# A mixture-of-experts router on four column tiles, and one transpose for a supertile's weights

## What is computed

```python
x = x + attn(layernorm(x))                 # latent attention, 64 sequences of 64 tokens, 8 heads
x = x + moe1(layernorm(x), ctx)            # 8 experts of width 512, top 2, routed by ctx
x = x + moe2(layernorm(x))                 # the part that the change touches

def moe2(h):                               # h: (4096, 128)
    scores = sigmoid(h @ gate_w.T)         # 32 experts
    sc = scores + gate_bias
    grp = sc.reshape(-1, 8, 4)             # 8 groups of 4; keep the 4 groups with the best top-2 sum
    gmask = one_hot(top_k(top_k(grp, 2).sum(-1), 4)).sum(1)
    tki = top_k(where(repeat(gmask, 4) > 0, sc, 0), 8)
    w = scores[tki]; w = w / (w.sum(-1) + 1e-20) * 2.5
    combine = (one_hot(tki, 32) * w).sum(1)          # (4096, 32)
    g, u = silu(h @ w_gate), h @ w_up                # every token through every expert, width 64
    routed = (g * u * combine) @ w_down
    return routed + silu(h @ sh_gate) * (h @ sh_up) @ sh_down   # a shared expert of width 128
```

## Time and profile before

| | |
|---|---|
| time, median of 3 runs | 756.46 us (754.01 to 759.85) |
| profiled execution | 756.52 us, of which 754.8 us from its first to its last instruction |
| TensorE busy | 669.3 us, 89% of the span |
| VectorE busy | 552.5 us, 73% |
| ScalarE, GpSimd busy | 353.1 us, 47%; 345.7 us, 46% |
| mean granted TensorE clock | 0.95 |
| second expert layer | from about 400 us to the end |

### The profile page before, as it was taken

One profiled execution on the slowest core, in us unless ns is written; L12 is line 12 of the kernel. 1 busy time (PEld: TensorE's weight loads), 2 busy tenths in 40 slices (PEclk: granted clock), 3 DMA queues, 4 the chain that ended last, 5 costly groups with the idle time before them and its releaser, 6 DMA issues.

```text
span 754.8 us, 11001 instructions
## 1 busy us (share of the span) xinstructions
PE 669.3 (89%) x3456; PEld 475.5 (63%) x3456; DVE 552.5 (73%) x1318; ACT 353.1 (47%) x628; POOL 345.7 (46%) x386
## 2 busy tenths in 40 slices
PE   6868999999708999999992988999999999999997
PEld 5535666666506777777771755666666666666664
DVE  4367877779517999999964786777868695958564
ACT  3844666655204666666663533444343424353221
POOL 5111377778867999999957324040312213000000
PEclk9967999999958999999997898999999999999999
DMA  9900300000023466666311293354555545444442
GB/s 227 366 11 0 92 30 29 29 29 34 38 77 88 127 206 193 179 188 193 113 56 45 59 207 87 90 154 109 132 112 138 129 112 132 111 130 112 124 116 58
DMA packets 73816, 84.14 MB, mean 111 GB/s; under 512 B 15057, under 2 KB 42683, under 8 KB 73758
## 3 DMA queue, kind: packets, MB, share of 16 engines
q1 hardware_dynamic: 68536, 74.93, 36.4%
q0 software_dynamic: 4096, 8.40, 3.8%
q10 hardware_dynamic: 1126, 0.11, 0.1%
HBM read 64.48 MB, written 18.87 MB: 110 GB/s over the span
## 4 chain that ended last, share of the span: by engine, by line
PE 57%; POOL 18%; DVE 11%; issue 7%; ACT 4%; DMA 2%; another core or an unknown queue 0%; SPq 0%; POOLq 0%; ACTq 0%; DVEq 0%
PE pair_banks L1625 15%; POOL h1h L586 7%; PE bank L1408 7%; PE bank L1410 6%; PE bank L1409 6%; POOL W2l L571 4%; PE pair_banks L1315 4%; PE score_banks L1410 3%; PE score_banks L1408 3%; PE score_banks L1409 3%; POOL W2h L566 3%; PE bank L1447 2%; PE pair_banks L1493 2%; POOL x_sorted L544 2%; PE bank L1467 2%
## 5 line engine op out<-in xcount | busy, mean ns | idle before, releaser
L865 ACT ACTIVATE r_s<-bank 128x512 f32<-128x512 f32 x136 | 81.1, 598 | 160.7 <-PE bank L1410 150.8
L1625 PE MATMUL pair_banks<-t_s,Dn 128*128 128x512 f32 x272 | 138.6, 595 | 0.0
L1150 DVE TENSOR_TENSOR h1l<-r,h1h 128x512 fp32r<-128x512 f32 x92 | 113.4, 1251 | 16.2 <-POOL h1h L586 16.2
L1408 PE MATMUL bank<-fxh,Gh 128*128 128x512 f32 x136 | 97.6, 718 | 0.0
L1265 DVE TENSOR_TENSOR rc_s<-r_s,score_banks 128x512 f32<-128x512 f32 x90 | 61.5, 684 | 49.0 <-ACT r_s L865 39.5
L1278 DVE TENSOR_TENSOR t_s<-rc_s,bcb 128x512 f32<-128x512 f32 x128 | 87.4, 685 | 4.1 <-DMA bcb<-c_rows 2.6
L586 POOL TENSOR_SCALAR h1h<-r 128x512 fp32r<-128x512 f32 x92 | 73.8, 806 | 19.6 <-ACT r L816 17.3
L605 POOL TENSOR_TENSOR mvp<-mvp,meps 128x4 f32<-128x4 f32 x8 | 1.6, 197 | 172.4 <-DVE mvp L1188 172.4
L544 POOL DMA_INDIRECT x_sorted<-xsb,posi x64 | 64.2, 1003 | 31.9 <-DVE xsb L1077 19.8
L597 POOL DMA_INDIRECT yg<-y_sorted,posi x64 | 64.3, 1005 | 25.3 <-issue 18.4
L1625 PEld LDWEIGHTS pair_banks<-t_s,Dn 128*128 128x128 f32 x272 | 51.4, 190 | 14.7 <-issue 3.8
(11 more groups left out here) (286 smaller groups left out, 1611.4 us busy)
## 6 DMA issues: line engine op xcount, KB each, us to landing
bcb<-c_rows SPq DMA_DIRECT2D x128, 256.0 KB
wraw<-in_L_xattn_W SPq DMA_DIRECT2D x46, 256.0 KB, 2.9
x_sorted<-wraw SPq DMA_DIRECT2D x1, 5888.0 KB, 17.4
xg<-x_sorted SPq DMA_DIRECT2D x23, 256.0 KB, 3.4
y_sorted<-ysb SPq DMA_DIRECT2D x23, 256.0 KB, 3.0
ctxb<-in_ctx SPq DMA_DIRECT2D x8, 256.0 KB, 6.0
out<-x_all SPq DMA_DIRECT2D x8, 256.0 KB
x_all<-in_x SPq DMA_DIRECT2D x2, 512.0 KB, 5.2
```

The costliest lines, as they stand in the source:

```text
L865: act.activation(r_s[:, n % RB2, :], bank[n % 3][:, :], ACT.Silu).then_inc(F["act"], 1)
L1150: tt(h1l[:, n % NB1, :], r1[:, n % RB1, :], h1h[:, n % NB1, :].bitcast(F32), ALU.subtract)\
L1408: mm(dst, wh, xh, start=start, stop=False)
L1625: mm(bank[6][:, :], Dn[:, weights_of(p), :], t_s[:, n % TB2, :], start=(p == 0), stop=(p == NC2 - 1))\
```

## The change

The router logits of the second layer take the form of the first router: `gwT` is stationary, tokens stream, the four tiles of a supertile go to four column tiles. The result, experts of four tiles on 128 rows by 128 tokens, is copied to SBUF (`lgS`, a new step of ScalarE), and turned by one transpose (`back`, a new step of TensorE) before the sigmoid. The routing weights `cw` (128 x 4 tiles x 32) are turned by one 128x128 transpose in place of four; `cT` is 128x128, and SP writes it to `c_rows` in four DMAs. In the tables, `sc` and the routing of supertiles 2 to 7 come one chunk later; supertile 1's `lg` comes one chunk later, `sc`, `rt_a` to `rt_d`, `c_ps` and `cT` two chunks later (`rt_a` from chunk 11 to 13, `c_ps` from 16 to 18, which is chunk 1 of supertile 1). In the first expert layer the bias load counts on the weights' semaphore.

```diff
-SLOTS = dict(cmbA=-5, cmbB=-4, paggr=-3, prstd=-2, pnb=-1, pxn=0, pxT_ps=2, pxT=2, fxl=3, lg=4, sc=5, rt_a=6, rt_b=7,
-             rt_c=8, rt_d=9, c_ps=14, cT=14, accS=8, tp=10, x2=12)
-
-
-FIRST = dict(cmbB=4, paggr=4, pnb=5, pxn=7, pxT_ps=9, pxT=9, fxl=10, lg=11, sc=11, rt_a=11, rt_b=12, rt_c=13, rt_d=14,
-             c_ps=16, cT=16)
+SLOTS = dict(cmbA=-5, cmbB=-4, paggr=-3, prstd=-2, pnb=-1, pxn=0, pxT_ps=2, pxT=2, fxl=3, lg=4, lgS=4, back=5, sc=6, rt_a=7,
+             rt_b=8, rt_c=9, rt_d=10, c_ps=14, cT=14, accS=8, tp=10, x2=12)
+
+
+FIRST = dict(cmbB=4, paggr=4, pnb=5, pxn=7, pxT_ps=9, pxT=9, fxl=10, lg=12, lgS=12, back=13, sc=13, rt_a=13, rt_b=14, rt_c=15,
+             rt_d=16, c_ps=18, cT=18)
...
-    steps = [(name, 1) for name, s in FIRST.items() if i == 0 and s == p]
+    steps = [(name, 1) for name, s in FIRST.items() if divmod(s, NC2) == (i, p)]
...
-            cT = a("cT", [E2, ST])
+            cT = a("cT", [P, P])
+            lgS = a("lgS", [P, P])
...
-                sp.dma_start(bcur[:, b % BB, :].unsqueeze(1), bT[:, ds(e, 1), :]).then_inc(s_b[b % BB], 16)
+                sp.dma_start(bcur[:, b % BB, :].unsqueeze(1), bT[:, ds(e, 1), :]).then_inc(s_w[b % WB], 16)
...
-                sp.dma_start(cs[j], cT[:, :]).then_inc(s_cs, 16)
-                sp.wait_ge(s_cs, 16 * (j + 1))
+                for t in range(TPS):
+                    sp.dma_start(cs[j][:, t * P:(t + 1) * P], cT[t * E2:(t + 1) * E2, :]).then_inc(s_cs, 16)
+                sp.wait_ge(s_cs, 16 * TPS * (j + 1))
...
-                    pool.wait_ge(s_w[b % WB], 32 * (b // WB + 1))
+                    pool.wait_ge(s_w[b % WB], 48 * (b // WB + 1))
...
+            def prep_lg(j):
+                act.wait_ge(F["lg"], j + 1)
+                copy(lgS[:, :], bank[7][:, 0:P]).then_inc(F["lgS"], 1)
+
             def prep_sc(j):
-                act.wait_ge(F["lg"], j + 1)
-                act.activation(scores[:, :, :], bank[7][:, 0:TPS * E2].rearrange("p (t e) -> p t e", t=TPS),
+                act.wait_ge(F["back"], j + 1)
+                act.activation(scores[:, :, :], bank[7][:, P:P + TPS * E2].rearrange("p (t e) -> p t e", t=TPS),
                                ACT.Sigmoid).then_inc(F["sc"], 1)
 
             def prep_c(j):
                 act.wait_ge(F["c_ps"], j + 1)
                 if j >= 1:
-                    act.wait_ge(s_cs, 16 * j)
-                copy(cT[:, :], bank[7][0:E2, :]).then_inc(F["cT"], 1)
+                    act.wait_ge(s_cs, 16 * TPS * j)
+                copy(cT[:, :], bank[7][:, 0:P]).then_inc(F["cT"], 1)
...
                 for t in range(TPS):
-                    ins = mm(bank[7][:, t * E2:(t + 1) * E2], xTt[:, t * P:(t + 1) * P], gwT[:, :],
+                    ins = mm(bank[7][t * E2:(t + 1) * E2, 0:P], gwT[:, :], xTt[:, t * P:(t + 1) * P],
                              start=True, stop=True)
                 ins.then_inc(F["lg"], 1)
+
+            def prep_back(j):
+                pe.wait_ge(F["lgS"], j + 1)
+                transpose(bank[7][:, P:2 * P], lgS[:, :]).then_inc(F["back"], 1)
 
             def prep_c(j):
...
-                for t in range(TPS):
-                    ins = transpose(bank[7][0:E2, t * P:(t + 1) * P], cw[:, t, :])
-                ins.then_inc(F["c_ps"], 1)
+                transpose(bank[7][:, 0:P], cw[:, :, :].rearrange("p t e -> p (t e)")).then_inc(F["c_ps"], 1)
 
             prep_x(0)
             prep_logits(0)
             pe.wait_ge(s_f2l, NG)
+            prep_back(0)
```

More of the change, by code:

```diff
@@ L299, in decoder_kernel @@
         s_w = [sem(f"expert_in{i}") for i in range(WB)]
-        s_b = [sem(f"expert_bias_in{i}") for i in range(BB)]
         s_xg = [sem(f"sorted_in{i}") for i in range(XB)]
@@ L323, in decoder_kernel @@
         F = {n: sem("f2_" + n) for n in (
-            "up gate act rc t dn accS tp x2 cmb1 cmb bst pstat prstd pnb pxn pxT_ps fxh xT fxl lg sc cw c_ps cT "
+            "up gate act rc t dn accS tp x2 cmb1 cmb bst pstat prstd pnb pxn pxT_ps fxh xT fxl lg lgS back sc cw c_ps cT "
             "chain").split()}
@@ L811, in _ @@
                 if c == 0:
-                    act.wait_ge(s_b[b % BB], 16 * (b // BB + 1))
+                    act.wait_ge(s_w[b % WB], 48 * (b // WB + 1))
                 act.wait_ge(B["up"], n + 1)
@@ L858, in _ @@
             prep_x(0)
+            prep_lg(0)
             prep_sc(0)
@@ L879, in _ @@
                             prep_x(j)
+                        if name == "lgS":
+                            prep_lg(j)
                         if name == "sc":
@@ L1676, in _ @@
                             prep_logits(j)
+                        if name == "back":
+                            prep_back(j)
                         if name == "c_ps":
```

## The result

| | before | after |
|---|---|---|
| median | 756.68 us (753.54 to 759.85, 15 runs) | 749.34 us (747.27 to 751.2, 15 runs) |
| profiled execution | 756.52 us, span 754.8 | 747.27 us, span 745.5 |
| TensorE busy, VectorE busy | 669.3, 552.5 us | 660.7, 552.1 us |
| first transpose of the second layer to the end | 342.40 us | 335.47 us |

The ratio is 0.9907 with an interval of 0.9889 to 0.9925: 7.0 us less, against 8.0 forecast. It is 0.93%, so by the bound of 1% named in the prediction "the same".

What follows compares the result with a forecast made beforehand. TensorE was taken to bound the second expert layer's steady part. From the profiled 756.5 us, -6.0 (chunk 18), +2.1 (clock) and -4.1 (steady supertiles) sum to -8.0: 748.5 us forecast, range 743.5 to 753.5.

Steps and rivals of the forecast that it cites:

- the hole before supertile 1's weights: TensorE's wait for VectorE's `cw` before transposing supertile 1's weights: 3.2 us in place of 5.1.
- the hole at 438: TensorE's idle time from 437.58 to 439.24, supertile 1's logits waiting for `fxl`: claimed to close.
- Chunk 18 earlier, -6.0: Second chunk of supertile 1: first product at 457.5 in place of 463.53, 6.0 us earlier.
- The clock, +2.1: TensorE's clock falls to half after the 3.2 us wait before supertile 1's weights, losing 1.7 to 2.9 us, taken as 2.1.
- Rival A: Clock holds through the shorter wait before supertile 1's weights, so no 2.1 us loss: 746.4 us, chance 0.17.
- Steady, -4.1: Supertiles 2 to 7: cheaper logits and transposes on TensorE save 0.68 us each, 4.1 us in all (3.2 to 4.9).
- Rival D: Column tiles and transposes save little, as switching from full width costs more: 750.9 us, or 752.6 with nothing saved; chance 0.08.
- First spread, d = +0.5: Supertile 0's routing weights, written and broadcast: net 0 to 1.0 us later, taken as 0.5, from three more write issues.
- Rival C: The four DMA writes run one after another, delaying the first spread by 4.0 us: 752.0 us, chance 0.07.
- Rival B: Wait before supertile 1's weights does not shrink, VectorE 2 us later through late gathers or broadcasts: 750.5 us, chance 0.14.
- Rival E: TensorE idles at each supertile's transpose back, waiting for ScalarE's late copy: slower, 759.7 us at 3.5 us lateness, chance 0.05.
- The bias semaphore: First expert layer: GpSimd's `w_high` waits for a third small load, three blocks ahead: costs nothing.

Runs made afterwards that it cites:

- before's second trace: The kernel before, unchanged, profiled once more: 751.07 us, 338.78 us from the second layer's first transpose to the end.
- the shift alone: Kernel before with only supertile 1's step table moved later (logits before chunk 12, transposes before 18), old logits and transposes kept: 750.59 us, ratio 0.998.
- the filler: Changed kernel with 23 unused 256-column products on TensorE before it waits for supertile 1's weights: 745.27 us, ratio 0.9912 to the kernel before.
- The run with doubled products: Changed kernel with the four column-tile logits products issued twice: steady supertile period 40.12 us in place of 39.90.
- the change again: The changed kernel, unaltered, run again on the second chip: 746.63 us, ratio 0.9932 to the kernel before.
- the two tables alone: Kernel before with supertile 1's steps shifted and later supertiles' combines behind the routing, old logits, transposes and single write kept: 745.38 us, ratio 0.9907.
- the later combine: Changed kernel with the combine of the next supertile but one, and preparation steps after it, moved behind the routing: 742.64 us, ratio 0.9883 to the kernel before.

## Why the prediction was right, and where its terms were off

The time lies 0.84 us above the forecast and within its range, and the mechanism is the one described: the hole before supertile 1's weights shrinks and does not close (3.2 forecast, 2.85 measured), the low clock follows it, the hole at 438 is gone, TensorE does not wait at the transpose back once the first supertile is under way (at the very start it does, for 0.48 us), and the steady period is shorter. That the number came out so well owes something to luck: on the second chip the same change is worth 5.1 us (3.5 to 6.8) and not 8.0, and the largest term holds against one of the two traces of the kernel before and not against the other. Term by term:

- **Chunk 18 earlier, -6.0.** -5.75 between the two first traces. The count along VectorE held to 0.3 us: 457.4 forecast for the transpose, 455.33 + 2.37 = 457.7 found. But the 5.1 us from which it was subtracted was one execution's, with the sigmoid 1.8 us late. Against before's second trace chunk 18 comes only 47.91 - 45.38 = 2.5 us earlier. This is the weakest step of the sum, and I had marked nothing of it as uncertain. I let VectorE's waits of 1.18 for `scores` and 0.73 for `r_s` disappear, and so had the weights only 1.3 us later. Against the first trace they are 1.6 later (43.74 to 45.30 after the first transpose), but in the second neither wait exists, and against it (41.73) they are 3.6 later. Two more chunks on VectorE then take back most of the 4.5 us that TensorE gets done meanwhile, which is also why the shift alone won next to nothing.
- **The clock, +2.1.** In the trace +1.32 up to chunk 20, and up to +0.5 more until chunk 24, where TensorE waits 0.7 us for `fxl` at 465.16. Against a trace with the clock held it is 2.4, by the filler 2.3. Rival A and the forecast were both right, each for some executions: over all traces, idle times before these weights of 2.28, 2.65, 2.79, 2.86 (twice), 3.10, 3.74 and 4.54 us (twice) went with a low clock, the one of 1.93 did not.
- **Steady, -4.1.** -3.0. The term that was mis-sized: 0.49 to 0.50 a supertile and not 0.68. The logits cost 0.55, where I took 0.3 to 0.4 from the first router's 0.036 for each half-instruction with 0.1 for going in and out. The product itself is cheaper (0.027); going in and out costs 0.33. Part of the 0.33 could not be seen in the earlier trace rows: from the 0.57 us of that group 16 x 0.027 leaves 0.14, and the remaining 0.2 lies ahead of a group's first product, which that stretch leaves out. The two lone transposes cost 0.12 and 0.17, within 0.11 to 0.2. The new sum of 0.84 lies 0.04 above my upper bound.
- **Rival D,** the switch between full width and tiles, was thus true in part. If all of the 0.33 is the two switches, each costs some 0.17 and not 0.05, still less than the 0.25 with which I priced that rival, and my reading that the earlier trace rows bound them at 0.1 was wrong. The Trainium skill, TensorEngine Tiling (Array Packing), Key Properties, says that a change of the tiling mode drains the engine. A fixed cost of 0.33 us a group agrees with it. The run with doubled products doesn't tell a drain from what else a group pays once, such as its first weight load.
- **First spread, d = +0.5.** Counted from the first transpose, the write comes 0.90 us earlier, the first broadcast 0.26 later, the first `t_s` with `bcb` 0.87 later (21.62 to 22.49). Right in sign, 0.4 short; but this start, too, differs between executions, from 21.50 to 22.71 over the traces with four writes and from 21.26 to 21.62 with the one write of before. Rival C (writes one after another) is out: 0.43 us an issue.
- **Rival B,** a gather that is late, appears as 0.29 us at 444.89 and no more; in the change again it is 0.62, with one write 1.59. **Rival E** did not come: behind the 0.48 us at supertile 0 (414.33) TensorE never waits for `lgS` in the change.
- **The bias semaphore.** Nothing, as said: from the first layer's first transpose to the second's it is 187.3 us before and 187.2 after.

What stays open: why the sigmoid was late in that execution; and whether the change is worth 7.0 us in the pair's runs and 5.1 on the second chip, or the same in both. The intervals, 5.7 to 8.4 and 3.5 to 6.8, overlap. Nor is it shown that the late sigmoid is common in the pair's runs of the kernel before, though their median of 756.68 us, against 751.0 to 751.7 elsewhere, would fit it.

## What to carry to other kernels

- A stall on an engine that runs its list in order is removed from the releaser's list: count what that engine does ahead of the awaited result, and move what nobody waits for yet behind it, far enough. Here the two tables alone, with the old form, gave as much as the whole change, and the later combine on top of the change gave another 4.0 us; moved two chunks only, it gave a loss.
- A hole that carries the largest term of a sum should be read in a second execution. If there is only one, look at what each releaser in the chain waited for; a wait without a named releaser is a warning, and the term's lower bound is the sum without it.
- A wait moves with the work that is put ahead of it. The shift put two chunks under VectorE's backlog, and two more chunks into it: alone it won 0.5 us in the layer. Parts of a change are not to be priced one by one when one lengthens the chain that another one covers.

## What the runs showed of the hardware

- The clock after a wait differs between executions of one kernel. After 1.93 us of idle time TensorE kept 1.00; after 2.28 us it started at 1.00 and fell to 0.50 (1.2 GHz) 1.1 us later. The low stretch ran from 456.4 to 459.8 there, and from 455.3 to 462.1 in the first trace of the kernel before, where it began within the wait. With 23 products with unused results in the wait it stayed at 2.4 GHz in the one trace taken, and the layer was 2.3 us shorter than in the trace where it fell.
- A group of small products between full-width ones: 0.33 us once, 0.027 us for each half-instruction of 128 columns. Of the 0.55 us of such a group more than half is the fixed part, so fewer groups would bring more here than fewer instructions in one. That was not tried.
- Four DMA writes issued in a row cost 0.43 us each on the issuing queue, and their landings overlap: from first write to first broadcast it is 2.80 us for four, 2.52 for one that carries the same four pieces, and 1.64 for the one of before.
- A delay of 2.7 us at the sigmoid, on an engine (ScalarE) that is busy less than half of the time, cost 4.2 us at the end (2.6 to 5.8): VectorE's list hangs on the sigmoid and TensorE on VectorE's list, and TensorE has nothing else to do there.
